# Router product of a gated attention and expert block: one 8-row product per chunk becomes four 32-row products in four column groups, with a new order on all engines

## Chip, cores, metric

One Trainium2 chip, one of its cores. The metric is the device time of one launch in microseconds (us), as a median of several runs. One more execution was profiled; its rows are shown below.

## The reference

x is 4 batches of 512 rows by 512, float32. A first part adds a gated attention map to a layer norm of x; a second part is a feed-forward block with 8 experts, of which each row uses two, and one shared expert.

```python
x = x + tanh(g_xattn) * xattn(ctx_512, layernorm(x))
x = x + tanh(g_ffn) * ffn(layernorm(x))

# xattn (h = ctx, adj = layernorm(x), 512 x 512 for each batch)
sim = einsum('bhnd,bhmd->bnm', Q, K) / (sqrt(d) * H)
threshold = top_k(sim, 153)[..., -1:]                 # of each row
A = sigmoid(sim) * (sim >= threshold)
A = (A + A^T) * 0.5
return (1 - gamma) * adj + gamma * A

# ffn, x as 2048 rows
shared = silu(x @ shared_gate_w) * (x @ shared_up_w) @ shared_down_w
logits = x @ router_w                                  # 512 -> 8
top_val, top_idx = top_k(logits, 2)
probs = zeros.at[rows, top_idx].set(sigmoid(top_val))
gate, up = split((probs.T[:, :, None] * x) @ gate_up_w)  # each expert
return shared + (silu(gate) * up @ down_w).sum(experts)
```

## The kernel before

Everything is float32. The kernel is written engine by engine: each engine (SP for the DMA queue, POOL, ACT, DVE, PE) has a list of calls of small functions, written out by hand or by a planner, and waits on semaphores between them. The order of the calls on an engine is the order of execution there; nothing reorders it. An argument b is a batch of 512 rows, i one of its four tiles of 128 rows, j a job of the feed-forward part, t a tile of 128 gathered rows.

For each batch the first part runs `turn_ctx`, `turn_q`, `sim_tile` (PE), then a search for the threshold of each row: five rounds of counts over sim, two tiles of four on DVE (`count`, `move`) and two on ACT (`sign`), then `last_count`, `best_below`, `threshold`, `check_search`, `mask_sim` on DVE. `turn_a` (PE) adds A and its transpose in PSUM, `add_adjacency` (DVE) adds it to x and takes statistics, POOL takes a root (`root_of_mixed`), `normal_in` and `normal` give the normalized rows x2, and `turn_x2` and `turned_x2` transpose them into xT.

The router then works on a whole batch. `route` (PE) multiplies the four chunks of 128 inner columns of xT with the router's weights: four products with 8 weight columns and 512 moving columns. The result is transposed, 8 x 512; `turned_logits` (ACT) copies it to SBUF, `turn_logits` (PE) turns it back in four transposes, and DVE goes on: `pick_experts`, `rank_tokens`, `one_hots`, `weigh_experts` (which gives the weights of a row, `payl`), `add_table`, `choose_columns`, `place_columns`, `read_plan`. `read_plan(0)` follows batches 0 and 1 and names the first 9 tiles of gathered rows, `read_plan(1)` follows batches 2 and 3 and names the other 30.

The feed-forward part is 55 jobs: 16 shared ones (one tile of a batch each) and 39 gathered ones. A job is `up(j)` (four products 128x128 by 128x512), `silu_of`, `gate`, `turn_h`, `turned_h`, `down(j)` (two products), `y_of` and an accumulating DMA to the output (`shared` or `scatter` on POOL). A gathered job also has `gather(t)` (POOL, an indirect DMA from the rows in DRAM), `turn_rows(t)` and `turned_rows(t)`. `gather(0)` waits for the plan and for the rows and payloads of batches 0 and 1 in DRAM. From job 27 on each round is `up(j)`, `turn_rows`, `down(j - 1)`, `turn_h(j)`.

By the page, a load of one expert's gate and up weights, a load of a batch of x, a store of its rows and a store of its output base move 1 MB each, a payload 16 KB.

PSUM has eight banks: front (2), turned_x, turned_h, down (2), gate_up (2). The router's result of batch 0 goes to turned_x, those of the others to front.

Of the kernel before, what the change touches and what calls it, by code (L numbers as in the profile page):

```python
# [16 lines left out]
P = 128  # L17
# [8 lines left out]
def flamingo_gated_block(nc, x, ctx_in, g_xattn, g_ffn, wq, wk, gamma_raw, router_w, gate_up_w, down_w,  # L26
# [6 lines left out]
    RT = N // P  # L33
    DC = D // P
# [55 lines left out]
    with ExitStack() as stack:  # L90
# [10 lines left out]
        w_rt = sb("w_rt", [P, DC, E])  # L101
# [95 lines left out]
        logitT = tmp[0:E, 0, :]  # L197
# [28 lines left out]
        zero_ready = sem("zero_ready")  # L226
        scal_ready = sem("scal_ready")
# [73 lines left out]
        rows_out = sem("rows_out")  # L301
        payload_out = sem("payload_out")
        base_out = sem("base_out")
# [11 lines left out]
        def _(sp):  # L315
# [3 lines left out]
            def load_x(b):  # L319
                if b >= 2:  # L320
                    sp.wait_ge(x2_ready, RT * (b - 1))
                    sp.wait_ge(base_out, 16 * (b - 1))
                sp.dma_start(xs[:, b % 2], x_v[b]).then_inc(x_in[b], 16)
# [12 lines left out]
            def store_rows(b):  # L336
                sp.wait_ge(x2_ready, RT * (b + 1))
                sp.dma_start(rows_v[b][:, :, 0:D], x2[:, :, :]).then_inc(rows_out, 16)

            def store_payload(b):  # L340
                sp.wait_ge(payload, b + 1)
                sp.dma_start(rows_v[b][:, :, D:ROW], payl[:, b % 2]).then_inc(payload_out, 16)

            def store_base(b):
                sp.wait_ge(at_used, RT * (b + 1))
                sp.dma_start(out_v[b], xs[:, b % 2]).then_inc(base_out, 16)
# [9 lines left out]
            def load_router():  # L356
                sp.dma_start(w_rt[:, :, :], router_w.rearrange("(c p) e -> p c e", p=P)).then_inc(rtw_in, 16)
# [10 lines left out]

            load_ctx(0)
            load_wqk()  # L370
            load_scalars()
            load_x(0)
            load_x(1)
            load_ctx(1)
            load_ctx(2)
            load_ctx(3)
            load_router()
            load_shared()
            store_zeros()
# [3 lines left out]
            load_dn(1)  # L383
            load_gu(2)
# [9 lines left out]
            store_base(0)  # L394
            load_gu(6)
            store_rows(0)
            store_rows(1)
            load_gu(7)
            load_x(2)
            store_base(1)  # L400
            store_payload(0)
            store_payload(1)
            load_x(3)
            store_rows(2)
            store_base(2)
# [4 lines left out]
            sp.wait_ge(rows_out, 16 * B)  # L410
            sp.wait_ge(payload_out, 16 * B)
            sp.wait_ge(base_out, 16 * B)
# [6 lines left out]
        def _(pool):  # L419
# [3 lines left out]
            def link(ins):  # L423
# [17 lines left out]
                   allow_small_or_imprecise_dtypes=True).then_inc(const_ready, 1)  # L441
            G.memset(zeros, 0.0).then_inc(zero_ready, 1)
# [13 lines left out]
            def shared(j):  # L456
                n = JOBS[j][1]
                pool.wait_ge(y_done, j + 1)
                pool.wait_ge(base_out, 16 * (n // RT + 1))
                G.dma_start(out_v[n // RT][:, n % RT], y_sb[:, j % 2], accum_op=ALU.add).then_inc(shared_out[j % 2], 16)  # L460

            def gather(t):
                if t == 0:
                    pool.wait_ge(plan_ready, 1)
                    pool.wait_ge(rows_out, 32)
                    pool.wait_ge(payload_out, 32)
                    pool.wait_ge(dummy_out, 32)
                if t == EARLY:
                    pool.wait_ge(plan_ready, 2)
                    pool.wait_ge(rows_out, 16 * B)  # L470
# [1263 lines left out]
```

## Time and profile before

| | |
|---|---|
| median of 3 runs | 440.01 us (438.99 to 441.61) |
| the profiled execution's own time | 438.85 us |
| its span, first to last instruction | 437.0 us |
| busy: PE / DVE / ACT / POOL | 395.8 / 186.8 / 184.1 / 130.9 us |
| granted clock of PE, mean | 0.961 |

### The profile page before, as it was taken

The numbers are of one execution on the slowest core, as the hardware profiler recorded it, in microseconds if no ns is written. First come the engines' busy times: TensorE is split into PE (matmuls) and PEld (weight loads), VectorE is DVE, ScalarE is ACT, GpSimd is POOL, SyncE is SP. The second block draws the span as 40 slices with busy tenths as digits, with TensorE's granted clock in tenths as the row PEclk, the third lists the DMA queues.
The fourth block names the chain that finished last, engine by engine and source line by source line (L and its number), as shares of the span: only waits on it lengthen the run. The fifth ranks groups of instructions, "written<-read, shape, count | busy, mean of one in ns | idle before, by whom it ended". The sixth has DMA issues, their size and how long they took to land.

```text
span 437.0 us, 4860 instructions
## 1 busy us (share of the span) xinstructions
PE 395.8 (91%) x1250; PEld 190.4 (44%) x1250; DVE 186.8 (43%) x711; ACT 184.1 (42%) x385; POOL 130.9 (30%) x122
## 2 busy tenths in 40 slices
PE   4907699999979999999999999999999999999980
PEld 2402354444445553455445444444544444444430
DVE  3899788589877668765162101111100111111000
ACT  2576369362556286263423333333333333323320
POOL 1110000010162153202223244444444443444221
PEclk9965989999989999999999999999999999999996
DMA  7999460144874085405716455555555555555332
GB/s 239 355 387 387 171 205 1 24 120 113 267 180 66 8 220 134 82 4 128 160 24 92 75 91 95 96 97 94 94 96 96 97 98 97 97 90 85 64 40 38
DMA packets 30466, 53.67 MB, mean 123 GB/s; under 512 B 4774, under 2 KB 8102, under 8 KB 30438
## 3 DMA queue, kind: packets, MB, share of 16 engines
q0 software_dynamic: 11040, 24.81, 33.1%
q1 hardware_dynamic: 19398, 28.53, 18.9%
q8 instruction: 12, 0.20, 0.2%
q14 instruction: 16, 0.13, 0.1%
HBM read 29.93 MB, written 23.40 MB: 122 GB/s over the span
## 4 chain that ended last, share of the span: by engine, by line
PE 80%; DVE 7%; DMA 6%; ACT 2%; issue 1%; SPq 1%; POOL 0%; POOLq 0%; ACTq 0%
PE gate_up L992 40%; PE down L1013 20%; PE turned_x L972 4%; PE front L903 3%; PE turned_h L1000 3%; PE front L917 2%; DMA out_dram<-y_sb,idx 2%; PE front L909 2%; DMA w_gu<-in_ctx_dram 2%; DVE ge_words L1313 1%; PE front L901 1%; DMA x_rows<-payl 1%; DMA xg<-x_rows,idx 1%; PE turned_h L886 1%; PE turned_x L917 1%
## 5 line engine op out<-in xcount | busy, mean ns | idle before, releaser
L992 PE MATMUL gate_up<-w_gu,xT 128*128 x312 | 141.0, 595 | 0.0
L491 POOL DMA_INDIRECT out_dram<-y_sb,idx x39 | 61.9, 1587 | 120.5 <-ACT y_sb L661 63.1
L1550 DVE SCALAR_TENSOR_TENSOR h<-gate_up,p_t,silu 128x256 f32<-128x256 f32 x39 | 18.9, 484 | 164.2 <-ACT silu L634 159.1
L992 PEld LDWEIGHTS gate_up<-w_gu,xT 128*128 128x128 f32 x312 | 56.9, 192 | 58.2 <-issue 58.2
L1013 PE MATMUL down<-w_dn,hT 128*128 x156 | 73.9, 596 | 0.9 <-ACT hT L643 0.9
L992 PE MATMUL gate_up<-w_shgu,xT 128*128 128x512 f32 x128 | 58.5, 600 | 0.0
L661 ACT ACTIVATE y_sb<-down,gates 128x512 f32<-128x512 f32 x55 | 37.7, 687 | 46.1 <-PE down L1013 38.5
L634 ACT ACTIVATE silu<-gate_up,p_t 128x256 f32<-128x256 f32 x39 | 18.5, 474 | 86.6 <-PE gate_up L992 86.6
L475 POOL DMA_INDIRECT xg<-x_rows,idx x39 | 39.7, 1019 | 34.6 <-DMA x_rows<-payl 18.1
L1013 PEld LDWEIGHTS down<-w_dn,hT 128*128 128x128 f32 x156 | 27.0, 190 | 24.4 <-issue 24.4
L992 PEld LDWEIGHTS gate_up<-w_shgu,xT 128*128 128x128 f32 x128 | 23.8, 193 | 25.8 <-issue 25.6
L460 POOL DMA_DIRECT2D out_dram<-y_sb x16 | 15.3, 977 | 51.6 <-ACT y_sb L661 51.6
L1013 PE MATMUL down<-w_shdn,hT 128*128 128x512 f32 x64 | 30.2, 596 | 0.0
L972 PEld LDWEIGHTS turned_x<-ident,xg 128*128 128x128 f32 x156 | 19.5, 143 | 22.7 <-issue 18.2
L652 ACT COPY xT<-turned_x 128x512 f32<-128x512 f32 x39 | 22.9, 587 | 12.4 <-PE turned_x L972 12.4
L972 PE MATMUL turned_x<-ident,xg 128*128 128x128 f32 x156 | 24.1, 278 | 3.0 <-DMA xg<-x_rows,idx 2.6
L643 ACT COPY hT<-turned_h 128x256 f32<-128x256 f32 x55 | 20.2, 367 | 12.1 <-PE turned_h L1000 10.7
L568 ACT ACTIVATE junk<-sim,probe 128x512 int8<-128x512 f32 x32 | 22.8, 716 | 5.2 <-DVE probe L1322 3.0
L1000 PEld LDWEIGHTS turned_h<-ident,h 128*128 128x128 f32 x110 | 15.0, 144 | 20.6 <-issue 19.7
L454 POOL TENSOR_TENSOR pow2out<-pow2in,half 128x4 f32<-128x4 f32 x4 | 4.1, 1030 | 62.7 <-DVE pow2in L1406 62.7
L600 ACT ACTIVATE x<-xs,x2add,pow2out 128x512 f32<-128x512 f32 x16 | 12.4, 809 | 24.5 <-DVE x2add L1410 24.5
L1313 DVE TENSOR_SCALAR_CACHE_REDUCE ge_words<-sim,probe 128x512 uint8<-128x512 f32 x32 | 22.5, 741 | 0.2
(175 smaller groups left out, 415.3 us busy)
## 6 DMA issues: line engine op xcount, KB each, us to landing
w_gu<-in_L_ffn_gate_up_w_dram SPq DMA_DIRECT2D x8, 1024.0 KB, 12.5
xs<-in_x_dram SPq DMA_DIRECT2D x4, 1024.0 KB, 7.7
w_dn<-in_L_ffn_down_w_dram SPq DMA_DIRECT2D x8, 512.0 KB, 12.7
out_dram<-xs SPq DMA_DIRECT2D x4, 1024.0 KB, 7.5
x_rows<-x SPq DMA_DIRECT2D x4, 1024.0 KB, 4.8
out_dram<-y_sb POOLq DMA_DIRECT2D x16, 256.0 KB, 4.1
w_gu<-in_ctx_dram SPq DMA_DIRECT2D x4, 256.0 KB, 8.2
xg<-x_rows,idx POOLq DMA_INDIRECT x39, 4.2
```

The source lines that it names most:

```text
L475: G.indirect_dma_start(out=xg[:, t % XG, :], out_offset=None, in_=x2_rows[0:2 * N, :] if t < EARLY else x2_rows[:, :], in_offset=bass.Indi ...
L491: G.indirect_dma_start(out=out[0:2 * N, :] if t < EARLY else out[:, :], out_offset=bass.IndirectOffsetOnAxis(ap=idx[:, t:t + 1], axis=0), ...
L568: ins = A.activation(junk[:, i - SHARE], sim[:, b, i], ACT.Sign, scale=-1.0, bias=probe[:, k, i:i + 1], accum_out=sgn[:, k, i:i + 1])
L643: A.copy(hT[:, j % 2], h_b[:, 0:I].rearrange("p (c t) -> p c t", c=IC)).then_inc(ht_done, 1)
L652: A.copy(xT[:, x_slot(j)], x_b[:, :].rearrange("p (c t) -> p c t", c=DC)).then_inc(xt_done, 1)
L661: A.activation(y_sb[:, j % 2], y_b[j % 2][:, :], ACT.Copy, scale=gates[:, 1:2]).then_inc(y_done, 1)
L972: mm = TE.transpose(x_b[:, c * P:(c + 1) * P], xg[:, t % XG, c * P:(c + 1) * P], ident[:, :])
L992: mm = TE.matmul(g_b[j % 2][:, :], xT[:, x_slot(j), c], w, start=(c == 0), stop=(c == DC - 1))
L1000: mm = TE.transpose(h_b[:, c * P:(c + 1) * P], h[:, c * P:(c + 1) * P], ident[:, :])
L1013: mm = TE.matmul(y_b[j % 2][:, :], hT[:, j % 2, c], w, start=(c == 0), stop=(c == IC - 1))
L1313: ins = V.tensor_scalar(ge[:, i], sim[:, b, i], probe[:, k, i:i + 1], None, ALU.is_ge, ALU.add, accum_out=cnt[:, k, i:i + 1])
L1550: V.scalar_tensor_tensor(h[:, :], g_b[j % 2][:, I:F2], p_t[:, t % XG:t % XG + 1], silu[:, :], ALU.mult, ALU.mult).then_inc(h_ready, 1)
```

## The change

The router's weights get 32 columns in place of 8; the 24 new ones are zero, written by POOL before the load. Each chunk of the product is now four instructions, one for each row tile of the batch, with 128 moving columns each; tile i writes the PSUM partitions 32i to 32i + 31 of one bank, which places it in column group i of the array. The result is 128 x 128, one transpose turns it back, and DVE picks 8 of each 32 columns.

```diff
-        w_rt = sb("w_rt", [P, DC, E])
+        w_rt = sb("w_rt", [P, DC, GRP])          # GRP = 32
...
-        logitT = tmp[0:E, 0, :]
+        logitT = tmp[:, 0, 0:P]
...
             def load_router():
-                sp.dma_start(w_rt[:, :, :], router_w...).then_inc(rtw_in, 16)
+                sp.wait_ge(wide_ready, 1)
+                sp.dma_start(w_rt[:, :, 0:E], router_w...).then_inc(rtw_in, 16)
...
+            G.memset(w_rt[:, :, :], 0.0).then_inc(wide_ready, 1)
...
-                A.copy(logitT, (x_b if b == 0 else f_b[0])[0:E, :]).then_inc(logitT_done, 1)
+                A.copy(logitT, (x_b if b == 0 else f_b[0])[:, 0:P]).then_inc(logitT_done, 1)
...
             def route(b):
                 pe.wait_ge(x2t_done, RT * (b + 1))
+                bank = x_b if b == 0 else f_b[0]
                 for c in range(DC):
-                    mm = TE.matmul((x_b if b == 0 else f_b[0])[0:E, :], w_rt[:, c, :], xT[:, :, c, :],
-                                   start=(c == 0), stop=(c == DC - 1))
+                    for i in range(RT):
+                        mm = TE.matmul(bank[i * GRP:(i + 1) * GRP, 0:P], w_rt[:, c, :], xT[:, i, c, :],
+                                       start=(c == 0), stop=(c == DC - 1))
...
             def turn_logits(b):
                 pe.wait_ge(logitT_done, b + 1)
-                for i in range(RT):
-                    mm = TE.transpose((x_b if b == 0 else f_b[1])[:, i * E:(i + 1) * E], logitT[:, i * P:(i + 1) * P],
-                                      ident[0:E, 0:E])
+                mm = TE.transpose((x_b if b == 0 else f_b[1])[:, 0:P], logitT, ident[:, :])
```

The semaphores of the stores of rows, payloads and of the output's base (`rows_out`, `payload_out`, `base_out`), each one counter for all batches before, are now one for each batch. And the order of the calls is new on all five engines, from the first load to about job 26; the loop from job 27 on is as before.

On PE the stretch from the first router product on shows both edits. These are rows of the program before: the `turn_a` of batch 1 ends, then the router product of batch 0 (L917), its transposes (L924), the `turn_x2` of batch 1 (L909), and the router product of batch 1.

```order
L901 MATMUL front<-ident,sim 128x128 x4
L903 MATMUL front<-sim,ident 128x512
L917 MATMUL turned_x<-xT,w_rt 8x512 x4
L1013 MATMUL down<-w_shdn,hT 128x512 x2
L924 MATMUL turned_x<-ident,tmp 128x8 x4
L909 MATMUL front<-ident,x 128x128 x8
L1013 MATMUL down<-w_shdn,hT 128x512 x2
L909 MATMUL front<-ident,x 128x128 x4
```

The same place in the changed program (L926 is the router product, L932 its transpose, L999 an `up`, L1020 a `down`):

```order
L908 MATMUL front<-ident,sim 128x128 x4
L910 MATMUL front<-sim,ident 128x512
L926 MATMUL turned_x<-xT,w_rt 32x128 x16
L999 MATMUL gate_up<-w_shgu,xT 128x512 x4
L932 MATMUL turned_x<-ident,tmp 128x128
L1020 MATMUL down<-w_shdn,hT 128x512 x2
L916 MATMUL front<-ident,x 128x128 x8
L1007 MATMUL turned_h<-ident,h 128x128 x2
```

Four instructions became sixteen, four transposes one, and an `up` (3) now stands between product and transpose, where a `down` stood.

On SP's queue this is the stretch from the output's base of batch 0 (L346) to the payloads of batches 0 and 1 (L342), before. L329 is a load of gate and up weights, L338 a store of normalized rows, L323 a load of x.

```order
L346 DMA out_dram<-xs 128x4x512
L329 DMA w_gu<-in_L_ffn_gate_up_w_dram 128x4x512
L338 DMA x_rows<-x 128x4x512 x2
L329 DMA w_gu<-in_L_ffn_gate_up_w_dram 128x4x512
L323 DMA xs<-in_x_dram 128x4x512
L346 DMA out_dram<-xs 128x4x512
L342 DMA x_rows<-payl 128x4x8 x2
L323 DMA xs<-in_x_dram 128x4x512
```

And in the changed program (L331 weights, L340 rows, L360 the router's weights, L348 base, L325 x, L344 payloads):

```order
L331 DMA w_gu<-in_L_ffn_gate_up_w_dram 128x4x512 x2
L340 DMA x_rows<-x 128x4x512
L360 DMA w_rt<-in_L_ffn_router_w_dram 128x4x8
L348 DMA out_dram<-xs 128x4x512 x2
L325 DMA xs<-in_x_dram 128x4x512 x2
L340 DMA x_rows<-x 128x4x512
L344 DMA x_rows<-payl 128x4x8 x2
L331 DMA w_gu<-in_L_ffn_gate_up_w_dram 128x4x512
```

The last weight load (expert 7), which waits for PE's `sim_tile(3, 3)`, stood ahead of a load of x, a base and the payloads, and now stands behind them; the router's weights, loaded near the start before, now come behind the rows of batch 0.

On DVE the start is changed too. Before, the statistics of batch 1 (L1295 to L1301, `sim_stats(1)`) stand between the fourth count and the fifth of batch 0:

```order
L1313 TENSOR_SCALAR ge_words,cnt<-sim,probe 128x512 x2
L1295 BN_STATS stats<-sim 128x6 x4
L1298 BN_AGGR mvs<-stats 128x2 x4
L1300 COPY mean<-mvs 128x4
L1301 TENSOR_SCALAR powin<-mvs 128x4
L1318 SCALAR_TENSOR_TENSOR u<-cnt,stride 128x2
L1320 SCALAR_TENSOR_TENSOR u<-sgn,stride 128x2
L1322 SCALAR_TENSOR_TENSOR probe<-u,probe 128x4
L1331 TENSOR_SCALAR ge_words,cnt<-sim,probe 128x512 x4
```

Now the fifth count (L1338) follows at once:

```order
L1320 TENSOR_SCALAR ge_words,cnt<-sim,probe 128x512 x2
L1325 SCALAR_TENSOR_TENSOR u<-cnt,stride 128x2
L1327 SCALAR_TENSOR_TENSOR u<-sgn,stride 128x2
L1329 SCALAR_TENSOR_TENSOR probe<-u,probe 128x4
L1338 TENSOR_SCALAR ge_words,cnt<-sim,probe 128x512 x4
```

`sim_stats(1)` stands behind `mask_sim(0)`, and two counts of batch 1 stand between `add_adjacency(0)` and `normal_in(0)`, which followed each other before. ACT's list of the same stretch now has the four `sign` of batch 0 without a copy between them. `weigh_experts(1)` comes before `choose_columns(0)` and `place_columns(0)`, where it came behind them.

## Rows read from the trace of the kernel before

**Rows 1.** The page: the chain that ended last, by engine.

```profile
PE 80%; DVE 7%; DMA 6%; ACT 2%; issue 1%; SPq 1%; POOL 0%; POOLq 0%; ACTq 0%
```

**Rows 2.** That chain in order of time, one late round: start us, us, what.

```profile
405.01 3.44 PE gate_up L992 x8
...
408.88 1.72 PE down L1013 x4
...
410.82 3.44 PE gate_up L992 x8
```

**Rows 3.** What PE waited for from 57 to 417 us: total, times, longest.

```profile
PE turned_x L972 <- DMA xg<-x_rows,idx: 2.6, 1, 2.6
PE front L917 <- ACT xT L611: 0.7, 1, 0.7
PE turned_x L972 <- ACT xT L652: 0.3, 1, 0.3
```

**Rows 4.** Timeline of PE around batch 0's router product: start, us, then the instruction.

```profile
83.83 3.60 PE L917 MATMUL turned_x<-xT,w_rt 128*8 128x512 f32 x8
87.36 1.98 PE L1013 MATMUL down<-w_shdn,hT 128*128 128x512 f32 x4
89.28 0.41 PE L924 MATMUL turned_x<-ident,tmp 8*128 8x8 f32 x4
89.61 1.09 PE L909 MATMUL front<-ident,x 128*128 128x128 f32 x8
...
92.76 0.18 PE L931 MATMUL turned_x<-mask,upper 128*128 128x32 bf16 x1
92.79 0.18 PE L932 MATMUL turned_x<-mpre,ones 128*128 128x32 bf16 x1
```

**Rows 5.** Timeline of PE's weight loads in the same product.

```profile
83.83 0.10 PEld L917 LDWEIGHTS turned_x<-xT,w_rt 128*8 128x8 f32 x2 [0.76 <-issue]
84.26 0.09 PEld L917 LDWEIGHTS turned_x<-xT,w_rt 128*8 128x8 f32 x1 [0.34 <-issue]
```

**Rows 6.** Groups by line: ACT's copy of the router's result, busy, mean ns.

```profile
L619 ACT COPY tmp<-front 8x512 f32<-8x512 f32 x3 | 1.7, 574 | 6.8 <-PE front L917 6.8
```

**Rows 7.** The chain in order of time at the first gathered rows.

```profile
112.01 5.34 DMA x_rows<-payl
...
118.30 4.34 DMA xg<-x_rows,idx
122.69 0.82 PE turned_x L972 x4
...
124.27 1.09 PE turned_x L972 x4
125.36 4.05 PE gate_up L992 x8
```

**Rows 8.** Timelines of SP's queue and of DVE ahead of that.

```profile
104.95 0.37 SPq L329 DMA_DIRECT2D w_gu<-in_L_ffn_gate_up_w_dram  x1
...
105.93 0.50 SPq L346 DMA_DIRECT2D out_dram<-xs  x1
...
113.36 0.21 DVE L1531 TENSOR_TENSOR oh_e<-front,iota 128x72 f32<-128x72 f32 x1
```

**Rows 9.** Timelines of DVE and PE in the first 61 us.

```profile
26.77 1.41 DVE L1295 BATCH_NORM_STATS2 stats<-sim 128x6 f32<-128x256 f32 x4
...
46.40 0.75 DVE L1394 SCALAR_TENSOR_TENSOR xs<-front,c,xs 128x512 f32<-128x512 f32 x1 [0.69 <-PE front L903]
...
53.89 0.16 DVE L1410 SCALAR_TENSOR_TENSOR x2add<-mv,pow2out 128x4 f32<-128x4 f32 x1 [1.12 <-POOL pow2out L454]
...
57.12 4.14 PE L992 MATMUL gate_up<-w_shgu,xT 128*128 128x512 f32 x8
```

**Rows 10.** Timelines of DVE and PE where batch 3's mask is used.

```profile
190.54 2.73 DVE L1386 SCALAR_TENSOR_TENSOR sim<-sim,thr,tmp 128x512 f32<-128x512 f32 x4
...
194.26 0.60 PE L901 MATMUL front<-ident,sim 128*128 128x128 f32 x4
```

More of the change, by code:

```diff
@@ L409, in _ @@
             store_payload(3)
-            sp.wait_ge(rows_out, 16 * B)
-            sp.wait_ge(payload_out, 16 * B)
-            sp.wait_ge(base_out, 16 * B)
+            for b in range(B):
+                sp.wait_ge(rows_out[b], 16)
+                sp.wait_ge(payload_out[b], 16)
+                sp.wait_ge(base_out[b], 16)
             sp.wait_ge(dummy_out, 32)
@@ L1042, in _ @@
             sim_tile(2, 2)
+            sim_tile(2, 3)
             turn_a(0, 0)
@@ L1049, in _ @@
             turn_a(0, 3)
-            sim_tile(2, 3)
+            sim_tile(3, 0)
             pe.wait_ge(at_used, 3)
@@ L1085, in _ @@
             route(0)
-            down(2)
+            up(3)
             turn_logits(0)
+            down(1)
             pe.wait_ge(at_used, 7)
@@ L1091, in _ @@
             turn_x2(1, 1)
-            down(3)
+            turn_h(2)
+            pe.wait_ge(logit_used, 1)
+            rank_pairs(0)
             pe.wait_ge(x2t_done, 5)
             turn_x2(1, 2)
-            pe.wait_ge(logit_used, 1)
-            rank_pairs(0)
             pe.wait_ge(x2t_done, 6)
             turn_x2(1, 3)
+            up(4)
+            turn_h(3)
             route(1)
@@ L1141, in _ @@
             turn_a(2, 1)
+            turn_rows(4)
             pe.wait_ge(at_used, 9)
@@ L1174, in _ @@
             table(2)
-            down(13)
-            down(14)
-            turn_rows(5)
+            turn_h(14)
+            up(15)
             up(16)
@@ L1180, in _ @@
             turn_h(15)
-            up(17)
-            turn_h(16)
-            down(15)
+            down(13)
+            turn_rows(7)
+            down(14)
             pe.wait_ge(table_used, 3)
@@ L1191, in _ @@
             turn_a(3, 3)
-            down(16)
-            up(18)
+            turn_h(16)
+            down(15)
+            up(17)
             pe.wait_ge(at_used, 15)
@@ L1197, in _ @@
             turn_x2(3, 1)
-            turn_h(17)
-            up(19)
+            up(18)
+            down(16)
             pe.wait_ge(x2t_done, 13)
@@ L1203, in _ @@
             turn_x2(3, 3)
-            turn_rows(7)
+            turn_h(17)
+            up(19)
+            route(3)
             turn_h(18)
-            route(3)
             down(17)
@@ L1229, in _ @@
             down(21)
+            turn_rows(10)
+            down(22)
             turn_h(23)
             up(24)
-            turn_rows(10)
-            down(22)
+            up(25)
+            turn_rows(11)
             turn_h(24)
-            up(25)
             down(23)
+            turn_h(25)
             up(26)
-            turn_h(25)
-            turn_rows(11)
             down(24)
@@ L1574, in _ @@
             count(0, 3)
-            sim_stats(1)
             move(0, 3)
@@ L1582, in _ @@
             mask_sim(0)
+            sim_stats(1)
+            add_adjacency(0)
+            first_probe(1)
             count(1, 0)
@@ L1585, in _ @@
             count(1, 1)
+            normal_in(0)
             move(1, 1)
-            add_adjacency(0)
-            normal_in(0)
+            sim_stats(2)
             count(1, 2)
-            sim_stats(2)
             move(1, 2)
+            row_affine(1)
             count(1, 3)
```

484 lines of the change are left out of this document (240 added, 244 removed).

## Prediction

> **What bounds the kernel now.** I read the chain that ended last first: 80% of the span is PE [rows 1], so work taken from PE shortens the run unless another engine becomes late. Its late part repeats: `up` of 3.44 us, `down` of 1.72, and the next `up` begins 5.81 us after the last [rows 2]. The two leave 0.65 us, which `turn_rows` and `turn_h` fill: PE has no gap there. Then I asked what PE waited for between its first `up` at 57.12 us [rows 9] and the end of its work: 2.6 us for the first gathered rows, 0.7 for xT at the router product of batch 1, 0.3 for a copy [rows 3]. So from 57 us on the kernel is a sum of PE's work with 3.6 us of waits, and everything before it is a chain of DVE, ACT and PE on batch 0. The work left behind the last product (last scatters) is not touched.
>
> **The router product.** Four instructions, eight records, take PE from 83.83 to 87.36 [rows 4]: 3.53 us, 0.43 a record of 512 columns and 0.09 at the change of shape. The weight load of each record begins with the record before it, 0.43 us apart, and takes 0.09 [rows 5]: it is hidden, though it fills the same rows of the array. There are four such products, 14.1 us in all, all of them in PE's packed stretch.
>
> After the change there are 16 instructions, 32 records of 128 columns, each 0.43 / 4 = 0.107 us if cost goes by columns. The trace has no product in several column groups, so I bound it. If all four groups run at once, 32 x 0.107 / 4 = 0.86 us. If none do, 32 x 0.107 = 3.43, as now. If besides each weight load is exposed, 32 x (0.107 + 0.09) = 6.3. I take a value between the first two, for one reason that the rows give: the two records of an instruction have the same output and so the same column group, and they stand next to each other. In order, the second can't begin before the first has streamed; only the second of one instruction and the first of the next can overlap. That is 16 x 0.107 = 1.71 us, and with a start of some 0.02 to 0.03 between neighbours (92.76 and 92.79 are two small products' starts [rows 4]) 16 x 0.025 more: 2.1 us with no further change of shape. So each product saves 3.53 - 2.1 = 1.4 us, **four save 5.7**.
>
> A rule speaks against this. The Trainium skill, page "TensorE: Matmul & The Clock Gate", section on packing small matmuls, says that a weight load overlaps with products in flight only where the row group differs. All 16 instructions here use all rows, so by that rule each load would stand alone; the loads just shown, hidden in the same row group, do not agree with it, and by the rule the product would be the 6.3 us case. The same section gives 2.38 times for three column groups with 512 columns; no run here shows it, and by that factor a product would be an estimated 3.43 / 2.38 = 1.4 us.
>
> **The transposes.** The `down` that starts at 87.36 streams 4 x 0.43 and ends at 89.08; the next transposes start at 89.61 [rows 4]. So four small transposes and two changes of shape cost 0.53 us. One 128 x 128 transpose: the 0.65 us above are six of them (four of `turn_rows`, two of `turn_h`), 0.11 each; with some slack 0.15. Saved 0.38, **four times 1.5 us**. ACT's copy takes 0.574 us for 8 x 512 [rows 6]; with 128 columns it can't be longer by anything that matters, and it lies under `up(3)` (3.44 us) for batch 0 and under `sim_tile(3, 2)` for batch 1, which is 0.86 us, two records of 0.43: enough. DVE's pick of 8 in 32 columns reads the same 128 x 32 values; nothing. POOL's memset of w_rt and the wait of the load on it come at the start, long before use; nothing, unless the load itself is late (below).
>
> **The wait for the first gathered rows.** The payload of batch 1 was issued at 112.01 and landed 5.34 us later, at 117.35; the gather began at 118.30, landed in 4.34 us and PE resumed at 122.69 [rows 7]. The plan was ready at about 113.6 (end of L1531 [rows 8]), so the payload was late by 3.8 us. It was late because SP had issued a weight load at 104.95, then a load of x and a base at 105.93 [rows 8], 3 MB, just ahead. Now base and x come earlier and the weight load later, and `weigh_experts(1)` stands before the column work, so the plan decides. PE waited 2.6 + 0.3 us here, and came back slow: the transposes took 0.82 and 1.09 where four cost 0.44, the `up` 4.05 instead of 3.44 [rows 7, 2]: 0.4 + 0.6 + 0.6 = 1.6. **Together 4.5 us.** What is late next: I went through the new lists by hand with the durations of the rows. PE was through at 122.69 - 2.6 = 120.1; less two products (2.8), two turns (0.76), the 0.7 told below, a `down` that now comes later (1.7), plus the 0.8 lost at the start and a `turn_h`, it arrives at 115.1; through the lists I get 114.1; the plan, bound by DVE's list (`one_hots(1)`, `count(2, 3)`, `gate(6)`, `move(2, 3)` stand ahead of `read_plan(0)`), is ready at some 110.0, plus 0.95 to start and 4.34 to land: 115.2. So 0.1 to 1.1 us of wait come back, **I take 0.6**, too short to slow PE much. The 0.7 us wait at batch 1's router product [rows 3] goes, as an `up` and a `turn_h` now lie ahead of it: **0.7**.
>
> **The start.** `sim_stats(1)` (1.41 and some 0.6 of small ones [rows 9]) leaves the chain of batch 0 and ACT's copies leave the search, so `add_adjacency(0)`, at 46.40 before [rows 9], begins some 3.5 us earlier. But then `normal_in(0)`, which only waited 1.12 us for POOL [rows 9], stands behind two counts and a move, 3.3 us, so 2.2 of this go back; and on ACT `sign(1, 3)` and `affine(1)` (4.3 us) stand ahead of `turned_x2(0, 1)`, for which `up(1)` waits. Following both lists, `up(0)` begins at about 56.6 (before 57.12) but PE then stands for 1.5 to 2 us before `up(1)`. Counting the same work, PE is behind by **0.8 us** when batch 1's `turn_a` ends. The router's weights are issued at about 67 and needed at 79; hidden, by 12 us less some 7 to land.
>
> **The second half.** The mask of batch 3 ended at 193.3, PE took it at 194.26 [rows 10]: one us of slack, with DVE waiting much for PE before. By hand through the new lists DVE and ACT keep up: 63 us of DVE work against 63.5 of PE's from the first `turn_rows` to that place, DVE starting 4.7 us ahead. I find a wait of 0.55 before the router product of batch 2 (ACT's signs and copies ahead of `turned_x2(2, 3)`) and 0.45 of small ones: **1.0 us lost**.
>
> **Sum.** 5.7 + 1.5 + 4.5 + 0.7 = 12.4 gained, 0.6 + 0.8 + 1.0 = 2.4 lost: 10.0 us less. The profiled execution took 438.85 us (its span 437.0 and 1.85 around it), so it would be 428.9; against the median of 440.01 it is 430.0. I say **429.2 us**, between them. A measurement of this kernel can tell about 0.5% (2.2 us) from no change.
>
> **Rivals.**
> - *All four groups overlap* (0.86 to 1.2 us a product). For it: nothing in the chip's rows forbids it; against it: the pair of records. Products 2 and 3 save 1 us more each; those of batches 0 and 1 bring PE earlier to a plan that DVE bounds, so little of theirs is kept: 427. Chance 0.2.
> - *No overlap* (3.5 us): the change of shape saves nothing in the product, and 4 x 1.4 come back, less the 0.6 us wait that PE then doesn't have: 5.7 - 0.6 = 5.1 more, 434. This is the case that the product does not do what it says. Chance 0.18.
> - *A stall in the new order*, at batch 2 or 3, where the slack was one us [rows 10], or at `up(1)`: one of the waits that I found is 4 us longer, and PE's clock falls behind it as at 122.69 (1.6 us): 5.6 more, 435. Chance 0.12.
> - *Slower: exposed loads.* The place is the router product. At 6.3 us each instead of 2.1 the four cost 16.8 us more, less the 0.6 of wait: 16.2, so 445. It decides from 2.1 + (10.0 + 0.6) / 4 = 4.8 us a product. Against it: hidden loads of the same row group [rows 5]. Chance 0.05.
> - The forecast: 0.45.
>
> **How the numbers follow.** 429.2 is the likeliest. The range reaches down to the first rival with all of its gain and a better start (424.5) and up past the second and third (436.5); what is left out is the slow case and the tails, under 2 in 10. Faster by over 0.5%: forecast, the first two rivals and most of the third, 0.90. Slower: the exposed loads and a part of the third, 0.06. Within: 0.04.
>
> **What would show it.** In the changed trace: the distance from the first record of L926 to PE's next instruction (2.1; 0.9, 3.5 or 6.3 for the rivals), and whether neighbouring records overlap in pairs; 0.15 us around L932; the payload landing within 2 to 3 us and the gather following the plan, with PE's wait at the first `turn_rows` below 1.1; `up(0)` near 56.6 with a pause of PE behind it; the late round still 5.81. The forecast is wrong if the product is outside 1.5 to 2.6 us, or if PE waits over 3 us in all beyond those that I named.

## The result, and the profile of the changed kernel

The changed kernel takes 423.26 us (median of 4 runs, 422.27 to 424.93), the one before, beside it, 439.5 us. The ratio is 0.963, 95% interval 0.958 to 0.968: 3.7% faster, 16.2 us. I had forecast 429.2 us, range 424.5 to 436.5. The direction was right, the gain was under-forecast by 6 us, and the time lies 1.2 us below the range. The profiled execution took 422.27 us, its span is 420.5 us (before 437.0).

The changed kernel's chain that ended last, by engine, answers to [rows 1]. PE has less of it and DVE more: up to 117 us the chain now runs over DVE's plan and the gathers instead of PE.

```profile
PE 75%; DVE 10%; ACT 5%; DMA 5%; issue 2%; POOL 1%; POOLq 0%; SPq 0%; DVEq 0%
```

The late round in the timeline of PE answers to [rows 2]. From one `up` to the next it is 249.34 - 243.53 = 5.81 us, as before:

```profile
243.53 3.60 PE L999 MATMUL gate_up<-w_gu,xT 128*128 x8
246.97 0.60 PE L979 MATMUL turned_x<-ident,xg 128*128 128x128 f32 x4
247.40 1.88 PE L1020 MATMUL down<-w_dn,hT 128*128 x4
249.12 0.38 PE L1007 MATMUL turned_h<-ident,h 128*128 128x128 f32 x2
249.34 3.17 PE L999 MATMUL gate_up<-w_gu,xT 128*128 x7
```

What PE waited for from 57 to 417 us, beside [rows 3]: no gathered rows of any length any more, and no xT at a router product. Of the 1.4 us at `down`, 0.9 stand in the last round at 406.8 us; the kernel before has the same 0.9 at 422.9, just outside this stretch.

```profile
PE down L1020 <- ACT hT L650: 1.4, 2, 0.9
PE gate_up L999 <- issue: 0.6, 1, 0.6
PE gate_up L999 <- ACT xT L618: 0.4, 1, 0.4
PE turned_x L938 <- DVE mpre L1441: 0.2, 1, 0.2
```

PE around batch 0's router product, and its weight loads there, beside [rows 4, 5]. From its first record to the next instruction the product takes 80.76 - 79.75 = 1.01 us, where it was 3.53. The one transpose of the logits, L932, stands between `up(3)`, whose eight records of 0.43 us from 80.76 on end at 84.2, and a `down` at 84.40: the turn costs 0.2 us where it was 0.53. The weight loads lie under the product again, with 0.81 us of busy time.

```profile
79.75 1.08 PE L926 MATMUL turned_x<-xT,w_rt 128*32 128x128 f32 x32
80.76 3.70 PE L999 MATMUL gate_up<-w_shgu,xT 128*128 128x512 f32 x8
84.29 0.27 PE L932 MATMUL turned_x<-ident,tmp 128*128 128x128 f32 x1
84.40 1.02 PE L1020 MATMUL down<-w_shdn,hT 128*128 128x512 f32 x2
...
79.74 0.81 PEld L926 LDWEIGHTS turned_x<-xT,w_rt 128*32 128x32 f32 x32 [0.76 <-issue]
```

The chain at the first gathered rows, then PE there, beside [rows 7]. The payload lands in 2.78 us instead of 5.34, ahead of the plan; POOL issues the first gather at 109.14, and PE takes the rows at 113.46. They landed at 113.41, and the `up` ahead of them was through its columns at 113.26, so 0.2 us of wait are left. In after_again (below), the same kernel once more, they landed at 112.62 and PE came at 113.28 without a wait.

```profile
104.26 0.20 DVE payl L1462
104.47 2.78 DMA x_rows<-payl
...
109.14 1.09 POOL xg L482
...
113.46 0.66 PE L979 MATMUL turned_x<-ident,xg 128*128 128x128 f32 x4
```

The start, timelines of DVE and PE, beside [rows 9]:

```profile
43.31 0.75 DVE L1401 SCALAR_TENSOR_TENSOR xs<-front,c,xs 128x512 f32<-128x512 f32 x1 [0.99 <-PE front L910]
...
53.32 0.16 DVE L1417 SCALAR_TENSOR_TENSOR x2add<-mv,pow2out 128x4 f32<-128x4 f32 x1
...
54.48 1.94 PE L916 MATMUL front<-ident,x 128*128 128x128 f32 x8 [6.52 <-ACT x L607]
...
57.02 5.13 PE L999 MATMUL gate_up<-w_shgu,xT 128*128 128x512 f32 x8 [0.60 <-issue]
62.59 3.67 PE L999 MATMUL gate_up<-w_shgu,xT 128*128 128x512 f32 x8 [0.45 <-ACT xT L618]
```

`add_adjacency(0)` begins 3.1 us earlier than before, but `normal_in(0)` only 0.6 us earlier and `up(0)` 0.1. `up(0)` takes 5.13 us where [rows 9] has 4.14: PE stood still for 6.5 us ahead of it (4.0 before), and the granted clock is 0.50, the lower of TensorE's two levels (1.2 of 2.4 GHz), from 54.5 to about 60 us; before it was 0.50 from 55 to 58 and 0.90 from 58 to 59. `up(1)` begins at 62.59, when ScalarE's copy of its rows is there; before it began at 61.97.

### The profile page after: what moved, and what is told of

Same layout as the page of the kernel before. It is cut to its first block, busy times and chain, and to the rows that moved or that the text cites. A ratio compares the mean times of both kernels' runs of the same rounds, so it can differ in the third digit from the quotient of the medians.

```text
span 420.5 us, 5035 instructions
## 1 busy us (share of the span) xinstructions
PE 382.3 (91%) x1334; PEld 189.2 (45%) x1334; DVE 185.4 (44%) x711; ACT 183.0 (44%) x385; POOL 132.3 (31%) x123
## 4 chain that ended last, share of the span: by engine, by line
PE 75%; DVE 10%; ACT 5%; DMA 5%; issue 2%; POOL 1%; POOLq 0%; SPq 0%; DVEq 0%
PE gate_up L999 38%; PE down L1020 19%; PE turned_x L979 4%; PE front L910 3%; PE turned_h L1007 3%; DVE ge_words L1320 2%; DMA out_dram<-y_sb,idx 2%; PE down L898 1%; PE front L908 1%; ACT xs L598 1%; PE front L916 1%; DMA xg<-x_rows,idx 1%; PE front L898 1%; DVE xs L1401 1%; PE turned_h L893 1%
## 5 line engine op out<-in xcount | busy, mean ns | idle before, releaser
L999 PE MATMUL gate_up<-w_gu,xT 128*128 x312 | 139.8, 592 | 0.0
L498 POOL DMA_INDIRECT out_dram<-y_sb,idx x39 | 63.0, 1616 | 129.8 <-ACT y_sb L668 79.2
L999 PEld LDWEIGHTS gate_up<-w_gu,xT 128*128 128x128 f32 x312 | 56.7, 190 | 58.8 <-issue 58.8
L1020 PE MATMUL down<-w_dn,hT 128*128 x156 | 73.4, 594 | 0.9 <-ACT hT L650 0.9
L999 PE MATMUL gate_up<-w_shgu,xT 128*128 128x512 f32 x128 | 59.4, 608 | 1.0 <-issue 0.6
L1020 PEld LDWEIGHTS down<-w_dn,hT 128*128 128x128 f32 x156 | 27.0, 190 | 22.2 <-issue 22.2
L999 PEld LDWEIGHTS gate_up<-w_shgu,xT 128*128 128x128 f32 x128 | 23.7, 195 | 26.8 <-issue 26.5
L1020 PE MATMUL down<-w_shdn,hT 128*128 128x512 f32 x64 | 30.4, 598 | 0.5 <-ACT hT L650 0.5
L465 POOL DMA_DIRECT2D out_dram<-y_sb x16 | 16.2, 1057 | 34.8 <-ACT y_sb L668 34.8
L1007 PE MATMUL turned_h<-ident,h 128*128 128x128 f32 x110 | 21.4, 276 | 0.0
```

The lines of the kernel that those rows point to most:

```text
L498: G.indirect_dma_start(out=out[0:2 * N, :] if t < EARLY else out[:, :], out_offset=bass.IndirectOffsetOnAxis(ap=idx[:, t:t + 1], axis=0), ...
L999: mm = TE.matmul(g_b[j % 2][:, :], xT[:, x_slot(j), c], w, start=(c == 0), stop=(c == DC - 1))
L1007: mm = TE.transpose(h_b[:, c * P:(c + 1) * P], h[:, c * P:(c + 1) * P], ident[:, :])
L1020: mm = TE.matmul(y_b[j % 2][:, :], hT[:, j % 2, c], w, start=(c == 0), stop=(c == IC - 1))
```

## The experiments

Ratios are to the kernel before, run beside each; the comparisons of kernels with each other go by these ratios or by medians from the same chip.

### How the product gets its 1.01 us: three experiments on its order and its groups

**tile_by_tile**

```diff
-                for c in range(DC):
-                    for i in range(RT):
+                for i in range(RT):
+                    for c in range(DC):
```

> The changed kernel with the two loops of the router product exchanged: the four instructions of one row tile, and so of one column group, stand side by side (eight records of one group in a row), and the four groups follow one another. The product in the changed kernel takes 1.01 us from the first record of L926 to the next instruction. Theory A, each column group takes its own records and all four run at once, with the issue looking ahead far enough: 1.0 us here too, and the time of the changed kernel within 0.5%. Theory B, records start in program order and overlap only with the neighbours of another group: the eight records of a group stand side by side, so 28 of 32 starts come 0.107 us after the one before, some 3.1 us, four times 2.1 us more, about 431 us against 423. Theory C, a record of 128 columns costs about 0.027 us in any order and any group: 1.0 us here too, which one_group tells from A.

**one_group**

```diff
-                for c in range(DC):
-                    for i in range(RT):
-                        mm = TE.matmul(bank[i * GRP:(i + 1) * GRP, 0:P], w_rt[:, c, :], xT[:, i, c, :],
+                for i in range(RT):
+                    for c in range(DC):
+                        mm = TE.matmul(bank[0:GRP, i * P:(i + 1) * P], w_rt[:, c, :], xT[:, i, c, :],
```

(the logits are copied as 32 x 512 and turned in four pieces)

> The changed kernel with all sixteen products in column group 0: each writes a 32x128 piece of a 32x512 result, and four transposes of 32x128 take the place of the one of 128x128. Theory A (column groups run at once): 32 records in one group at 0.107 us, 3.4 us a product, the old price of 3.53, and transposes at the old 0.53 instead of 0.2; (2.4 + 0.33) x 4 = 11 us more, 434 us, less what a wait of PE absorbs. Theory C (a small tile is cheap by itself): 1.0 us a product, 424.6 us with the transposes.

**two_groups**

```diff
+                for m in range(2):
+                    for c in range(DC):
+                        for g in range(2):
+                            i = 2 * m + g
+                            mm = TE.matmul(bank[g * GRP:(g + 1) * GRP, m * P:(m + 1) * P], w_rt[:, c, :],
```

> The changed kernel with two column groups: row tiles 0 and 1, then 2 and 3, into a 64x256 result, two transposes of 64x128. Theory A: 16 records in each group at 0.107 us, 1.7 to 1.8 us a product, transposes about 0.3; 4 x (0.8 + 0.1) = 3.6 us more than the changed kernel, 427 us. Theory C: 1.0 us and no difference of over 0.5%. The model of my prediction (only the pair of neighbours overlaps, the two records of an instruction in order) gives 2.1 us here as it did for four groups, 428 us.

Measured: tile_by_tile 428.68 us (ratio 0.976, 0.972 to 0.979), one_group 435.6 (0.992, 0.989 to 0.995), two_groups 427.92 (0.973, 0.970 to 0.976). Batch 0's product in the chain in order of time of the three, in that order:

```profile
80.40 2.39 PE turned_x L926 x32
```

```profile
80.49 3.61 PE turned_x L926 x32
```

```profile
81.63 1.87 PE turned_x L928 x32
```

The same 32 records with the same columns take 3.61, 1.87 and 1.01 us in one, two and four column groups. A 128-column record is not cheap by itself (theory C falls); its cost is 0.109 us, and groups run beside each other (theory A). Theory A's times, 434 us for one_group and 427 for two_groups, were 1.6 and 0.9 us short. But theory A had 1.0 us for tile_by_tile as well, and it took 2.39, between A and B. How long a record waits behind others is seen in the starts of the single records, in ns from the product's first, as read from the three traces:

```
changed kernel  0 7 14 20 | 134 140 147 154 | 243 249 256 263 | ... | 789 795 802 809, next instruction 1011
tile_by_tile    0 134 243 352 461 | 467 570 600 679 709 789 819 928 | 934 1037 1067 ... | 1400 ... 2189, next 2391
one_group       0 133 242 351 461 570 ... 3408, next 3611
```

In the changed kernel, the four records of a burst start 7 ns apart and a burst follows 109 ns behind the last (134 the first time). The trace doesn't name a record's group; since records of one group never start closer than 109 ns in one_group, a burst is one record of each group. In tile_by_tile the second group begins at 467, just behind the first group's fifth of eight records (461); the third at 934, behind the second's fifth (928); the fourth at 1400. So there was a limit on how far a later group gets past waiting records. Two rules give these numbers: a look-ahead over four waiting records in all, or a queue of its own for each group that holds one record at work and three behind it. With a queue of five the second group could have begun at 352. The next run tells the two rules apart.

**pairs**

```diff
-                for c in range(DC):
+                for c0 in range(0, DC, 2):
                     for i in range(RT):
-                        mm = TE.matmul(bank[i * GRP:(i + 1) * GRP, 0:P], w_rt[:, c, :], xT[:, i, c, :],
+                        for c in (c0, c0 + 1):
```

> The changed kernel with the router product's instructions in another order: two of one row tile (four records of one column group) side by side, then two of the next, twice over. The starts in the run with the tiles one behind the other (2.39 us; a second group began when the first one's fifth of eight records began, so with three of its own still waiting) and in the changed kernel (1.01 us) fit one rule: a record waits only for its own column group, and the engine looks no further than four waiting records. Worked through for this order with 0.109 us a record, that rule gives 1.26 us to the last start's end, and 0.1 more as in the other two orders: 1.4 us, +0.4 x 4 = 1.5 us, 425 us. A look-ahead of two records gives 2.1 us (428 us), of eight 1.1 us (423.8 us).

Measured: 424.16 us, ratio 0.965 (0.962 to 0.968), the changed kernel's own within the intervals. The chain's row of the product:

```profile
80.99 1.05 PE turned_x L927 x32
```

Its records start at 0 14 27 40 | 134 147 160 174 | 243 ... : the fourth group's first record starts 40 ns in, though three records of each of the three groups ahead are still waiting, nine in all. A look-ahead of four in all is refuted, and what I expected (1.4 us) with it. The look-ahead of eight, to which I gave 1.1 us, comes near this run but is refuted by tile_by_tile, where the second group stood behind seven waiting records. Four records of one group fit side by side without holding up the next group, eight don't: a queue of four for each group fits all five orders that were run. Orders with five to seven side by side were not tried.

### Whether the product and the order add up

**product_only** and **order_only**: the diff in two halves. The first has the padded weights, the product, the one transpose and DVE's pick, with every list of before; the second has every list of the change with the old product. **after_again** is the changed kernel beside them.

```diff
 # product_only, on the kernel before
-                    mm = TE.matmul((x_b if b == 0 else f_b[0])[0:E, :], w_rt[:, c, :], xT[:, :, c, :],
+                    for i in range(RT):
+                        mm = TE.matmul(bank[i * GRP:(i + 1) * GRP, 0:P], w_rt[:, c, :], xT[:, i, c, :],
```

```diff
 # order_only, on the changed kernel
-                    for i in range(RT):
-                        mm = TE.matmul(bank[i * GRP:(i + 1) * GRP, 0:P], w_rt[:, c, :], xT[:, i, c, :],
+                    mm = TE.matmul((x_b if b == 0 else f_b[0])[0:E, :], w_rt[:, c, :], xT[:, :, c, :],
```

> The kernel before with the new router product, its one transpose and the padded columns, and every order (the engines' and the transfers') as before. If the parts of the change add up, four products save 2.5 us each and four turns 0.33 each, 11.4 us; but the first two products stand ahead of the first gathered rows, whose wait of 4.5 us is set by the payload and not by PE, and at the 0.7 us of the batch-1 route PE waits for ScalarE. Theory A with that wait: the first two products save nothing behind the wait but what the plan itself comes earlier by, so 6 to 9 us less than before, 431 to 434 us, with a wait at the first gathered rows above 4.5 us if the payload is late by its own issue. Rival: all 11.4 us come through, 428 us, since the payload's issue moves forward with PE.

> The kernel before with every order of the changed one (engines and transfers), and the old router product in 8 columns with its four transposes. If the order alone gives what my sum gave it (3.9 at the gathered rows, 0.7 at the batch-1 route, less 0.8 at the start): 3.8 us less than before, 436 us. If the order is worth what is left of the 16.5 us when 11.4 are taken away: 5 us less, 434.5 us. Rival: the order was laid out for a 1 us product, and with 3.5 us products it brings waits of its own: 439 us, no gain.

> The changed kernel once more beside the other two, to have all three on one chip: 423 us, 3.7% below the kernel before. If product_only and order_only together save as much as it does, the parts add up; if less, they help each other (one wait needs both).

| kernel | us | ratio to before (440.55 us) | less than before |
|---|---|---|---|
| product_only | 437.78 | 0.993 (0.989 to 0.997) | 2.8 |
| order_only | 434.03 | 0.984 (0.982 to 0.986) | 6.5 |
| after_again | 423.41 | 0.961 (0.959 to 0.963) | 17.1 |

The halves give 9.3 us, the whole 17.1: they need each other. What PE waited for from 60 us on in product_only:

```profile
PE front L935 <- DVE mpre L1438: 4.5, 2, 2.3
PE turned_x L976 <- DMA xg<-x_rows,idx: 2.1, 1, 2.1
PE front L913 <- ACT x L604: 1.9, 1, 1.9
PE front L923 <- ACT xT L615: 0.7, 1, 0.7
```

and in order_only from 60 to 417:

```profile
PE down L1017 <- ACT hT L647: 0.5, 1, 0.5
PE front L905 <- DVE sim L1390: 0.3, 1, 0.3
PE front L913 <- ACT x L604: 0.2, 1, 0.2
```

With the old lists PE is through with the product earlier and stands at the next places: at `rank_pairs` for the experts' masks of DVE (2.3 us, twice), at the normalized rows, and at the gathered rows still: 10.0 us in all with two shorter waits, where the kernel before has 3.8. Its granted clock is lower too, 0.96 from 80 to 120 us and 0.98 from 145 to 240, where the kernel before has 1.00 in both. The new lists put other PE work there, and without the new product they already take away nearly every wait.

### The payload's way, and the transfers

**payload_late**

```diff
             store_base(0)
-            store_base(1)
-            load_x(2)
-            load_x(3)
             store_rows(1)
+            load_gu(7)
+            load_x(2)
+            store_base(1)
             store_payload(0)
             store_payload(1)
-            load_gu(7)
+            load_x(3)
```

> The changed kernel, with the order of SP's transfers behind the first two batches set back to that of before: the payloads (16 bytes a row) stand behind a 1 MB store, a 1 MB load and the like again, and nothing else is moved. Theory D, the 4.5 us that the kernel before waited at the first gathered rows came from the payload's slow landing in traffic: the payload lands over 5 us after its issue, the gather starts 2.5 us or more later, PE waits 2 to 4 us at the first gathered rows, and with a lower clock behind it the time is 3 to 4.5 us longer, 427 us. Rival E, the wait went away since the plan (DVE) ends earlier against PE in the new order: PE waits under 1 us and the time stays within 0.5%.

Measured: 429.68 us, ratio 0.979 (0.973 to 0.984). The changed kernel's ratios are 0.963 and, in after_again, 0.961, with intervals apart from this one: 7 to 8 us less. The spans of the profiles, 427.8 and 420.5, are 7.3 us apart. The chain in order of time, and then the timeline of PE:

```profile
105.18 0.20 DVE payl L1462
105.39 9.01 DMA x_rows<-payl
...
115.38 4.02 DMA xg<-x_rows,idx
```

```profile
119.44 1.12 PE L979 MATMUL turned_x<-ident,xg 128*128 128x128 f32 x4 [5.10 <-DMA xg<-x_rows,idx]
120.35 2.80 PE L1020 MATMUL down<-w_shdn,hT 128*128 128x512 f32 x4
122.99 0.60 PE L979 MATMUL turned_x<-ident,xg 128*128 128x128 f32 x4
```

The payload (32 bytes a row, not the 16 of what I expected) takes 9.01 us instead of 2.78, and PE waits 5.1 us. Behind the wait the granted clock is 0.50, the lower level, from 119.44 to 122 us, and 1.00 from 123 on. From start to next start, the four transposes take 0.91 us and the `down` 2.64, where the changed kernel's take 0.49 and 1.72. Together 5.1 + 0.4 + 0.9 = 6.4 of the 7.3 us; the other 0.9 is there before the wait (PE is through with its `up` at 114.2 instead of 113.3). Theory D holds, at a higher price than its 3 to 4.5 us, and E falls. The payload is later here than in the kernel before (9.01 us against 5.34), so the run shows that the order of the transfers matters, not what it is worth in the change.

**transfers_only** and **late_transfers2**: the new product with all engines' lists of before and SP's new list, once from the start and once only behind `load_gu(5)`. The second's edit on product_only:

```diff
             load_gu(5)
-            store_base(0)
             load_gu(6)
             store_rows(0)
-            store_rows(1)
-            load_gu(7)
+            store_base(0)
+            store_base(1)
             load_x(2)
-            store_base(1)
+            load_x(3)
+            store_rows(1)
             store_payload(0)
             store_payload(1)
-            load_x(3)
+            load_gu(7)
```

> The new product with the new order of SP's transfers and every engine's instructions in the order of before. With every order of before, the new product gained 2.8 us instead of 11.4, and PE waited 2.1 us at the first gathered rows (payload 6.3 us on its way), 4.5 us at rank_pairs for the experts' masks of DVE, 1.9 us more at the normalized rows. Theory F, the lost gain is split between the payload's way and the engines' order: the payload lands in about 3 us, the wait at the first gathered rows is gone, and the other two stay, 6.4 us; 434 us. Theory G, the transfers are what held the gain back: all waits go, 428 us. Theory H, the payload's way was not the limit (another wait takes the place of the 2.1 us): 437 us.

> The new product with every engine's order of before, SP's transfers of the start as before, and only those behind load_gu(5) in the new order (both base stores, both loads of x, the rows, then the payloads, then load_gu(7)). The run with all transfers in the new order lost 5.4 us at the start (first shared job at 62.7 us instead of 57.1), which hid what its later part does. Theory F, the payload's way held back a part: it lands in 2 to 3 us instead of 6.3, the wait of 2.1 us at the first gathered rows goes and some clock comes back, while the 4.1 to 4.5 us at rank_pairs and the 1.9 us at the normalized rows stay; 434 to 435 us beside 437.8 with the old order of transfers. Theory H, the engines' order holds the plan back and PE is slowed elsewhere: no gain over 437.8 us.

Measured: transfers_only 438.75 us (0.998, 0.995 to 1.001), late_transfers2 435.66 (431.74 to 438.0; 0.991, 0.987 to 0.994). Theories F and G of transfers_only (434 and 428) miss. In the first the new start of SP's list does not suit the old lists: the first normalized rows are turned at 60.60 and the first `up` begins at 62.67 us, so nothing of it is a verdict on the payload. In the second, what PE waited for from 46 us on is

```profile
PE front L916 <- ACT x L607: 5.9, 2, 4.0
PE front L938 <- DVE mpre L1441: 4.1, 2, 2.3
PE front L926 <- ACT xT L618: 0.7, 1, 0.7
PE turned_x L979 <- ACT xT L659: 0.5, 1, 0.5
PE front L950 <- DVE msumx L1507: 0.5, 1, 0.5
```

Of the first row, 4.0 us are the pause ahead of the first normalized rows, which the kernel before has too. The DMA to landing of the payloads of batches 0 and 1, in product_only and here:

```profile
DMA to landing us min/median/max: 6.3/7.5/8.8
```

```profile
DMA to landing us min/median/max: 1.8/1.8/1.8
```

The wait for gathered rows is gone and the two others stay, which is theory F's picture. By the ratios its time is 1.1 us below product_only's, but their intervals overlap, so a gain is not shown, and theory H (no gain) stays open beside F.

### A shorter start

**early_x2**: on the changed kernel, `normal_in(0)` directly behind the first count of batch 1, and on ScalarE the first two normalized tiles and their turned copies ahead of all or most of the later sign passes. **early_x2_b2**: the third and fourth as well ahead of `affine(1)`.

```diff
 # DVE
             count(1, 0)
+            normal_in(0)
             move(1, 0)
             count(1, 1)
-            normal_in(0)
+            sim_stats(2)
             move(1, 1)
-            sim_stats(2)
 # ACT
             sign(1, 0)
-            sign(1, 1)
             normal(0, 0)
             normal(0, 1)
-            sign(1, 2)
             turned_x2(0, 0)
+            sign(1, 1)
+            turned_x2(0, 1)
+            sign(1, 2)
             sign(1, 3)
             affine(1)
-            turned_x2(0, 1)
```

> The changed kernel with a shorter way to its first shared job. PE idles 6.5 us from 48 us on for the first normalized rows, whose DVE step stands behind two counts of the batch-1 search, and whose copy on ScalarE stands behind a sign pass. Here DVE's normal_in(0) comes right behind the first count, ScalarE makes the two normalized tiles and their turned copies ahead of the later sign passes, and the statistics of batch 2 fill DVE's wait. Expected: the first gate and up product starts near 54.1 to 55 us instead of 57.0. Theory I, PE bounds the stretch behind: 2 us less, 421.4 us. Rival J, DVE's chain to the plan of the gathered rows (ended at 108.9 us, with 94% of DVE busy from 80 us on) is the true bound and PE, earlier by 2 us, waits for the gathered rows instead: no gain, 423 us, with a wait of some 2 us there.

> The run with the earlier first shared job (its first gate and up product at 53.6 us instead of 57.0) waited 3.5 us again at 61.8 us, for the third normalized tile, which stood on ScalarE behind the affine step of batch 1 (2.8 us) and two more steps; it ended 2 us behind the changed kernel. Here the third and fourth normalized tiles stand ahead of that step. Theory I, ScalarE's place of these tiles was what gave the gain away: the second wait is under 1 us and the time is 421 us. Rival J, with ScalarE and DVE at these loads, whatever is moved forward pushes back the search of batch 1 or the mask of batch 1, and PE waits there: 423 to 426 us, no gain over the changed kernel.

Measured: early_x2 425.17 us (ratio 0.968, 0.965 to 0.970), early_x2_b2 423.85 (0.963, 0.959 to 0.968): neither beats the changed kernel (0.961 and 0.963). In early_x2 neither theory holds: it takes neither 421.4 us nor is there a wait of 2 us at the gathered rows (0.5 at most). PE in the first and then in the second:

```profile
53.64 8.14 PE L999 MATMUL gate_up<-w_shgu,xT 128*128 128x512 f32 x16
65.31 0.64 PE L916 MATMUL front<-ident,x 128*128 128x128 f32 x4 [3.53 <-ACT x L607]
```

```profile
53.01 8.13 PE L999 MATMUL gate_up<-w_shgu,xT 128*128 128x512 f32 x16
...
66.30 3.78 PE L1020 MATMUL down<-w_shdn,hT 128*128 128x512 f32 x4 [3.22 <-ACT hT L650]
```

The first `up` begins 3.4 and 4.0 us earlier, and PE stands still again 8 to 10 us later, for another of ScalarE's steps. The mean granted clock from 57 to 80 us is 0.85 in both, against 0.94 and 0.90 in the two profiles of the changed kernel; in early_x2 it is 0.50, the lower level, from 68 to 72 us, behind the second pause. In the second run the wait for the normalized tile is gone, but another of 3.2 us stands in its place and the time is not 421, so theory I falls. J's time holds, not its place: PE waits for ScalarE's copy of h, and for batch 1's mask only 0.5 us. In these two orders, moving ScalarE's steps about shifts the pause.

## Why the forecast was too small, step by step

- **The router product** is the step that failed: "the two records of an instruction have the same output and so the same column group, and they stand next to each other. In order, the second can't begin before the first has streamed; only the second of one instruction and the first of the next can overlap." That made 2.1 us; it is 1.01, and 2.52 x 4 = 10.1 us are saved instead of 5.7. The second record does wait for the first, but the records of other groups do not wait behind it (bursts of four, and in pairs they pass nine waiting records). With two groups the model also gives 2.1 and the product took 1.87, but not in the model's way: the second group's first record starts 7 ns in, past the first group's waiting second record. That the number is near there is chance.
- **The rival that had this** (all four groups overlap, 0.86 to 1.2 us) was priced at 427, since the first two products "bring PE earlier to a plan that DVE bounds, so little of theirs is kept". That failed too. The first gather's issue on POOL moved with the product. It is this row in the chain of tile_by_tile, and the next one in that of one_group:

```profile
112.35 1.09 POOL xg L482
```

```profile
115.57 1.10 POOL xg L482
```

  The changed kernel has 109.14. With two products ahead of it, each 1.38 and 2.60 us longer, that is 3.2 and 6.4 us later for 2.8 and 5.2 of product (in one_group also 0.5 for two dearer turns). From 80 to 120 us DVE waited for the logits 0.4 us in the changed kernel, 3.0 and 5.9 in those. So the plan follows the product at least one for one, and full prices hold: the ratios of tile_by_tile and the changed kernel, 0.9756 and 0.9631, are 5.5 us of 439.4 apart, and 4 x 1.38 = 5.5. tile_by_tile is also nearly the forecast's case, with a product of 2.39 us against 2.1: at 2.1 its 428.7 would be an estimated 427.5, inside the range and 1.7 us below the forecast. So it is the product's size that carries the time out of the range.
- **The rule against the change.** The Trainium skill, page "TensorE: Matmul & The Clock Gate", section on packing small matmuls, has a weight load overlap with products in flight only where the row group differs. Here, 32 loads of one row group lie inside a product of 1.01 us, 0.81 us busy; measured, no load is exposed, so the slower rival (6.3 us) falls.
- **The transposes**: 0.33 x 4 = 1.3 us saved, forecast 1.5.
- **The gathered rows**: 4.5 and the 0.7 at batch 1's product are gone, as forecast. The mechanism at the gathered rows is the one forecast: payload_late brings a wait back there, and late_transfers2 takes it away with the old lists. Of the 0.6 to come back, 0.2 did: PE was through at 113.26 and the rows landed at 113.41, where I had 114.1 and 115.2. The forecast's 0.82 and 1.09 for slow transposes are pieces of the chain, which end with a record; from start to next start they were 0.61 and 0.88, and with a slow `turn_h` (0.47 instead of 0.22) the 1.6 us come out as 1.5, nearly the same.
- **The start**: `up(0)` at 57.02 where I had 56.6; batch 0's product starts 1.5 us later than the same work before (79.75, against the 83.83 of [rows 4] less an `up`, a `down` and two `turn_h` that now lie behind it: 3.44 + 1.72 + 0.44 = 5.6), forecast 0.8. The pause ahead of `up(1)` is 0.4 us, not 1.5 to 2, but `up(1)` does wait for ScalarE's copy, as forecast, and begins at 62.59, within 56.6 + 3.44 (or 4.1) + 1.5 to 2: the slow clock stretched `up(0)` over most of the pause. The term was too small by 0.7: `up(1)` lost 0.6 us against before, and 0.5 are a wait at `down(0)` for ScalarE's copy of h that I had not named.
- **The second half**: 1.0 us of loss was forecast; the three products behind batch 0 start without a wait, and of the rest 0.1 us is seen, at batch 2's mask (0.8 there in after_again's profile).

Sum by the trace: 10.1 + 1.3 + 4.5 + 0.7 - 0.2 - 1.5 = 14.9 of the 16.5 us between the spans; the cause of the other 1.6 us stays open. The terms off from the forecast: 4.4 for the product, 1.0 for the second half, 0.4 for the gathered rows, 1.6 unassigned, less 0.7 at the start and 0.2 for the transposes: 6.5, which is the miss in the span. That the halves need each other was not in the forecast at all: it added terms of the product and of the order, and such a sum comes near the measured time only because both were changed together.

## What to carry to other kernels

When small products share an operand but not an output, give each its own column group of the array and issue them in turn; look at the starts of single records, not at busy time, to see whether they run side by side. When a step on the busiest engine is shortened, the lists of the others have to be laid out for its new place: done alone, most of it turned into waits and a lower clock (2.8 of 11.4 us kept). A small transfer that a later step needs should be issued ahead of the big ones, not right behind them.

## What the runs showed of the hardware

- Records of different column groups run at once: 32 float32 records of 128 columns take 3.61 us in one group, 1.87 in two, 1.01 in four. Within a group they start 109 ns apart.
- Eight records of one group side by side held up the records of the next group until three of the eight were left waiting; four side by side held up none.
- A 16 KB store took 1.7 to 4.0 us to land where the large transfers were issued 11 us or more before it, or after it, and 5.3 to 12.2 us where three of 1 MB were issued 0.5 to 6 us before it (the payloads of batches 0 and 1 in the kernel before, product_only and payload_late).
- A pause of PE cost more than its length: behind the 5.1 us of wait in payload_late, the granted clock was 0.50; the four transposes and the first two records of `down` took twice as long (0.22 and 0.86 us each instead of 0.11 and 0.43), and in all 1.3 us were added.
